# Turning k with 32x32 block transposes on VectorE and sixteen transfers, in place of two TensorE transposes

## The reference

```
q, k = rotary(x @ Wq), rotary(x @ Wk);  v = x @ Wv;  g = silu(x @ Wg)
per chunk of 64 tokens:  attn  = (q @ k.T) * decay          # k is contracted over its 64 columns
                         o     = attn @ v + (q * cross_q) @ S
                         S_new = gamma^64 * S + (k * cross_k).T @ v
x1  = layernorm(x + (rmsnorm(o) * gn_weight * g) @ Wo)
out = layernorm(x1 + (silu(x1 @ Wgate) * (x1 @ Wup)) @ Wdown)    # integer weights times 1/127, hidden width 768
```

## Time and profile before

| | value |
|---|---|
| median of three runs | 423.6 us |
| the profiled execution's own time | 423.2 us |
| its span (first to last instruction) | 421.5 us |
| PE busy | 412.1 us (98%), 4698 matmuls |
| DVE busy | 313.2 us (74%), 912 instructions |
| ACT busy | 268.2 us (64%) |
| POOL busy | 183.2 us (43%) |
| packets of the SP transfer queue q1 | 14144, 19.08 MB |

### The profile page before, as it was taken

The page is one execution under the profiler, slowest core; times in us unless marked ns, Lnnn a source line. Parts: engine busy times, 40 slices in busy tenths (PEclk is TensorE's granted clock), DMA queues, the critical chain, the costliest instruction groups (busy, mean ns, idle before and its releaser), DMA issues.

```text
span 421.5 us, 12747 instructions
## 1 busy us (share of the span) xinstructions
PE 412.1 (98%) x4698; PEld 394.4 (94%) x4698; DVE 313.2 (74%) x912; ACT 268.2 (64%) x812; POOL 183.2 (43%) x330
## 2 busy tenths in 40 slices
PE   8999999998999999999999999999999999999994
PEld 6899999998999999999999999999999999998994
DVE  4999776677777777867777867777777777784975
ACT  6678655577666766766766766666666666654551
POOL 2532344355344455334355344445443434442654
PEclk9999999999999999999999999999999999999999
DMA  8931010101020201102020110201110010100001
GB/s 284 360 131 52 0 51 2 53 14 39 12 68 2 76 2 40 39 2 77 2 55 25 40 40 2 76 2 40 39 26 29 2 51 2 40 14 15 15 25 55
DMA packets 14352, 19.99 MB, mean 47 GB/s; under 512 B 1488, under 2 KB 9808, under 8 KB 14288
## 3 DMA queue, kind: packets, MB, share of 16 engines
q1 hardware_dynamic: 14144, 19.08, 14.1%
q10 hardware_dynamic: 144, 0.07, 0.1%
HBM read 14.94 MB, written 4.19 MB: 45 GB/s over the span
## 4 chain that ended last, share of the span: by engine, by line
PE 94%; DVE 2%; DMA 1%; issue 1%; POOL 1%; ACT 0%; SPq 0%; POOLq 0%; DVEq 0%; ACTq 0%
PE b_rows L527 30%; PE b_rows L545 20%; PE b_ffn L527 20%; PE b_turn L763 3%; PE b_head L793 3%; PE b_head L801 3%; PE b_turn L558 2%; PE b_state L820 2%; PE b_ffn L711 2%; PE b_head L722 2%; PE b_head L814 1%; PE b_rows L541 1%; DMA wf_int<-in_w_proj 1%; PE b_head L689 1%; PE b_head L685 1%
## 5 line engine op out<-in xcount | busy, mean ns | idle before, releaser
L2032 POOL TENSOR_TENSOR h_lo<-wf_int,h_hi 128x256 fp32r<-128x256 f32 x96 | 70.0, 742 | 121.7 <-ACT h_hi L1210 121.7
L527 PE MATMUL b_ffn<-x1T_hi,wf_hi 128*128 128x256 f32 x384 | 92.0, 279 | 0.1
L527 PE MATMUL b_ffn<-x1T_lo,wf_hi 128*128 128x256 f32 x384 | 91.5, 278 | 0.0
L1199 ACT ACTIVATE wf_int<-b_ffn 128x256 f32<-128x256 f32 x96 | 36.9, 384 | 59.5 <-PE b_ffn L527 59.4
L527 PEld LDWEIGHTS b_ffn<-x1T_hi,wf_hi 128*128 128x128 f32 x384 | 72.2, 188 | 0.6 <-DVE x1T_lo L1668 0.2
L527 PEld LDWEIGHTS b_ffn<-x1T_lo,wf_hi 128*128 128x128 f32 x384 | 72.2, 188 | 0.0
L545 PE MATMUL b_rows<-wp_hi,xT_hi 128*128 128x256 f32 x230 | 66.4, 289 | 1.2 <-issue 1.2
L545 PE MATMUL b_rows<-wp_hi,xT_lo 128*128 128x256 f32 x244 | 66.5, 277 | 0.0
L545 PE MATMUL b_rows<-wp_lo,xT_hi 128*128 128x256 f32 x230 | 63.8, 277 | 0.0
L1608 DVE TENSOR_TENSOR wf_int<-b_ffn,wf_int 128x256 f32<-128x256 f32 x96 | 40.2, 419 | 26.3 <-ACT wf_int L1199 25.7
L1186 ACT ACTIVATE sq<-b_head 128x128 f32<-128x128 f32 x120 | 33.3, 278 | 28.7 <-PE b_head L801 19.6
(11 more groups left out here) (191 smaller groups left out, 1166.5 us busy)
## 6 DMA issues: line engine op xcount, KB each, us to landing
xT_raw<-in_xT SPq DMA_DIRECT2D x16, 256.0 KB, 2.8
x_sb<-in_x SPq DMA_DIRECT2D x16, 256.0 KB, 3.0
out<-wf_int SPq DMA_DIRECT2D x30, 128.0 KB, 1.8
wf_int<-in_w_ffn SPq DMA_DIRECT2D x6, 384.0 KB, 6.7
wf_int<-in_w_proj SPq DMA_DIRECT2D x6, 256.0 KB, 4.7
rope_sb<-in_rope SPq DMA_DIRECT2D x4, 256.0 KB, 5.7
rope_q<-in_rope_by_row SPq DMA_DIRECT2D x2, 512.0 KB, 9.5
wo_raw<-in_w_o SPq DMA_DIRECT2D x1, 512.0 KB, 6.4
```

The lines of the kernel that those rows point to most:

```text
L527: mm = pe.matmul(dst, a, b, start=(i == 0 and j == 0 and not begun), stop=(i == n - 1 and j == len(passes) - 1 and not more), skip_group_c ...
L1199: act.activation(act_g[:, u], b_ffn[u][:, 0:256], ACT.Silu, scale=SCALE).then_inc(silu_done[j], 1)
L2032: pool.tensor_tensor(h_lo[:, ring, hb], h_full[:, u], h_hi[:, ring, hb].bitcast(F32), ALU.subtract).then_inc(h_split[j], 1)
```

## The change

Tiles 9 to 30 (`moved`) no longer go through PE and ACT. Right behind `sum_k`, DVE transposes each 32x32 block of k in place in the grid of blocks, into a new buffer `k_blocks` (a part of a buffer that is free by then). SP then issues sixteen transfers inside SBUF for each tile, one for each pair of source quadrant i and destination quadrant j, that put the blocks where the turned k wants them. Each transfer reads 32 partitions and writes 32 partitions, with two runs of 32 elements (128 bytes) in each. `heads_ready` waits for all sixteen. `turn_qk` and `keep_qk` fall away for these tiles; `turn_y` loses its wait for the copy, except in two places; `sum_k` loses its wait for `qkT_done`; and the DVE transpose waits until the sixteen transfers of the tile before have landed.

```diff
+        k_blocks = wf_int[:, 5 * 512:5 * 512 + 256].bitcast(F32)
+        def moved(n):
+            return PACKED <= n < NT - 1
+        def moves(n):
+            return 16 * (P // BLOCK) ** 2 * (n - PACKED + 1)
+        def turned_before(n):
+            return min(n, PACKED)
...
+            def move_k(n):                                   # SP
+                blocks = k_blocks.rearrange("p (b j c) -> p b j c", b=2, c=BLOCK)
+                sp.wait_ge(k_blocked, n - PACKED + 1)
+                sp.wait_ge(scores_done, n)
+                for i in range(P // BLOCK):
+                    src = slice(i * BLOCK, (i + 1) * BLOCK)
+                    for j in range(P // BLOCK):
+                        sp.dma_start(qkT[j * BLOCK:(j + 1) * BLOCK, 2:4, src], blocks[src, :, j, :]).then_inc(k_moved, 16)
...
                 slot(s, s // TS, s % TS)                     # SP, s in range(NT)
+                if moved(s):
+                    move_k(s)
...
                     if n + 3 > PACKED:                       # turn_y
-                        pe.wait_ge(qkT_kept, min(n + 3, NT))
+                        if n + 3 == PACKED + 1 or n + 3 >= NT:
+                            pe.wait_ge(qkT_kept, turned_before(n + 3) + (1 if n + 3 >= NT else 0))
...
                 n, m = s - 1, s - 2                          # heads_ready
-                pe.wait_ge(qkT_kept, n + 1)
+                if moved(n):
+                    pe.wait_ge(k_moved, moves(n))
+                else:
+                    pe.wait_ge(qkT_kept, turned_before(n) + 1)
...
-                turn_qk(s, q, t)                             # PE, end of packed_slot
+                if not moved(s):
+                    turn_qk(s, q, t)
...
-                if exists(n):                                # ACT, keep_qk
-                    act.wait_ge(qkT_done, n + 1)
+                if exists(n) and not moved(n):
+                    act.wait_ge(qkT_done, turned_before(n) + 1)
...
-                    dve.wait_ge(qkT_done, s - 1)             # DVE, sum_k
+                    if not moved(s - 2):
+                        dve.wait_ge(qkT_done, s - 1)
...
+            def block_k(n):                                  # DVE
+                dve.wait_ge(rotated, n + 1)
+                if n > PACKED:
+                    dve.wait_ge(k_moved, moves(n - 1))
+                dve.transpose(k_blocks, qk[:, n % 2, 256:512]).then_inc(k_blocked, 1)
...
                 sum_k(s, q, t)                               # DVE, packed_slot
+                if moved(s):
+                    block_k(s)
                 add_q(s, q, t)
```

More of the change, by code:

```diff
@@ L57 @@
 CHUNKED = PACKED - 1
+BLOCK = 32
 def rope_tables():
@@ L229, in build_block @@
         qkT_done, qkT_kept = sem("qkT_done"), sem("qkT_kept")
+        k_blocked, k_moved = sem("k_blocked"), sem("k_moved")
         v_copied, g_gated = sem("v_copied"), sem("g_gated")
```

## The result

| | before | after |
|---|---|---|
| median, 4 runs each | 423.76 us (423.06 to 424.33) | 520.39 us (517.3 to 522.82) |
| span of the profiled execution | 421.5 us | 515.6 us |
| mean granted clock of TensorE | 1.00 in the packed stage | 0.91 in the packed stage, 0.931 over the span |

The ratio is 1.2277, with a 95% interval of 1.2193 to 1.2362: 96.6 us slower. The prediction was 435.0 us, at most 450. The sign and the way in which the time is lost were forecast; the size was not: 96.6 us against the 11.4 of the forecast, more than eight times as much.

The account below looks back on a forecast made before the run. PE was taken to bound the kernel, with k's longer way stalling it 0.68 us in most slots. 16.28 us of stalls added less 4.84 removed gave +11.4, so 435.0 us; range 418.5 to 450.

Parts of the forecast that it names:

- Sixteen issues: SP issuing a tile's transfers: 0.43 us for the first, then 14 x 0.48 = 6.72 us to the sixteenth's start.
- d: Distance between starts of successive transfer issues on SP: taken as 0.48 us, ends 0.39 and 0.54.
- landing: Last transfer of a tile, from the start of its issue until it lands: 1.5 us, ends 1.2 and 2.1.
- first issue: SP's opening transfer of each tile's burst: 0.39 + 0.04 = 0.43 us.
- L: Time along k's way from one gate (PE's wait before `attention_out`'s last matmul) to the next: 12.93 us against 12.25.
- block transpose: DVE's added transpose of k behind `sum_k`, 128x256 float32: 0.42 us.
- last semaphore: From the last transfer's semaphore to the weight load on PE at the gate: 0.1 us.
- The removed transposes: Two PE transposes of L558 per tile, 0.22 us a slot, 22 tiles: 4.84 us gained, all on the path.
- Gate to `sum_k`: From PE's weight load for `attention_out`'s last matmul to the end of `sum_k` on DVE: 3.69 us.
- B: Rival: each SP issue pays twice for its second loop, 0.535 us apart; +28.4, about 452 us; chance 0.20.
- C: Rival: SP issue cost goes with rows, some 0.40 us apart; burst hidden, kernel faster, about 419 us; chance 0.19.
- D: Rival: issues about 0.45 us apart, stall eats the gain, within 3 us of before; chance 0.11.

Follow-up runs that it names:

- sixteen stores: Changed kernel with its sixteen transfers per tile aimed at an HBM scratch buffer instead of `qkT`, turned k of tiles 9 to 30 left out: 452.59 us, ratio 1.0692.
- PE kept busy: Changed kernel with fourteen matmuls on a constant operand put on PE ahead of the wait for the moves: 507.68 us, ratio 1.198.
- the first two experiments: Changed kernel without the sixteen transfers and their waits (420.15 us), and with only the eight of source quadrants 0 and 1 (420.17 us).

## Why the prediction was right in sign and wrong in size

The step that failed is **"Sixteen issues"**: d was taken as 0.48 us with ends of 0.39 and 0.54, and it is 0.597 for the issue and 0.04 behind it, 0.638 from start to start. All rows that it was read from the earlier trace rows are transfers with one end in HBM. The arithmetic on them was sound (the sixteen stores measured 0.47), but the prediction argued about rows and loops, and neither matters; the end that did differ, SBUF on both sides, was noted for the landing ("No transfer inside SBUF is in this trace") and not for the issue. Its range of d was narrow because it varied the wrong property. The stated ends of 0.39 and 0.54 do not hold 0.638. This step alone, with the first issue 2.41 us a slot or 53 us, turns the forecast of 435 into 488; stretched issues, clock and landing make up the rest.

The mean slot, term by term:

| term | us |
|---|---|
| L as predicted | 12.93 |
| distance of issues, 14 x (0.638 - 0.48) | 2.21 |
| first issue, 0.59 + 0.04 for 0.43 | 0.20 |
| landing, 1.78 for 1.5 | 0.28 |
| stretched issues, 11.6 us / 22 | 0.53 |
| lower clock between gate and `sum_k` (4.20 - 3.67, the means without and with PE kept busy) | 0.53 |
| sum | 16.68 |
| measured | 16.74 |

Twenty-two times 16.74 - 12.93 is 84 us; with the +11.4 of the prediction that is about 95, and 96.6 were measured. The experiment with PE kept busy gives the term of the clock a second time: its slots last 16.22 us in the mean, 0.52 less. Two small terms nearly cancel: the block transpose, 0.445 for 0.42, and the last semaphore, 0.04 us for 0.1. No row of the trace before had shown the 0.1.

- **The removed transposes**, 4.84 us: 3.8 measured (2.7 to 4.8), by the kernel without transfers. Its slots last 12.26 us for 12.45. The two pieces are gone, but sixteen matmuls of `gate_up` take 1.89 us in place of 1.81 in nine of its packed slots, and did so in two before. Why was not tried.
- **L against PE's slot, and a stall in each slot if L is longer**: right, shown by eight transfers (420.17), twelve (451.99) and sixteen (520.4). The chain after has each step in the order given. The point from which it decides, 0.431 us for sixteen, was not met by a run; by number of transfers it lies between eight and twelve, and both sides were seen.
- **The block transpose at 0.42 us**: 0.445, and free of cost by the first two experiments, since both run at the 12.26 to 12.29 us of a PE that never waits. So were the later `add_q` and `mask`; the loads of `xT` and `x` were nobody's wait.
- **Gate to `sum_k`, 3.69 us**: right only at full clock (4.20 us in the mean of the changed kernel). "PE's stop would not shorten it" holds, but the stop lengthened it, because the clock fell in the gap and the first matmuls behind it ran up to twice as long. The prediction did not ask what an engine does after it has stood still.
- **The rivals.** B had the direction (dearer issues) with the wrong cause and too low a price, 0.535. C and D needed 0.45 or less, which not even a burst with one end in HBM has (0.47); the 0.427 us that the prediction gives beside C is met by issues with one end in HBM (0.427 to 0.432 without the gap) and by none inside SBUF. The dearest case that had a sum came to 452 us, since none had a price outside the rows; all of the bad ends together, over 470, were left out of the range, and even they come to an estimated 473 by its own terms.
- **Stretched issues** stand in no term of the sum, though the trace of before has one: the 1608 ns in the earlier trace rows, which the prediction did not weigh. While SP was idle most of the time they cost nothing; in a chain that runs through SP each counts in full.

## What to carry to other kernels

Where many small transfers come between a producer and its consumer, count issues first: the issuing time of the burst, and not its bytes, is the length of the path, and a burst is free only while this path is shorter than the work that covers it. A price read from transfers with an end in HBM does not hold for transfers inside SBUF; if a kind of operation is not in the trace, list what differs (place, rows, loops) and let each widen the range. And when a change can make TensorE stand still, price the work just behind the gap at the lower clock, and see whether a few larger transfers by way of HBM do the same with less.

## What the runs showed of the hardware

- An issue on SP takes 0.43 us back to back with one end in HBM and 0.59 to 0.62 us with both in SBUF, for 32 or 128 partitions and one or two runs; about 0.04 us lie between two. The Trainium skill (DMA: Bandwidth & Descriptors, Why small descriptors are slow (HBM only)) excepts transfers inside SBUF from its penalty on small descriptors. No run here measures that bandwidth; in the issue itself they are the dearer ones.
- SP and ACT issue at the same time without slowing each other noticeably: eight each in 5.07 and 5.41 us, with medians of 0.64 and 0.65 us from start to start, against 0.64 for SP alone.
- Now and then an issue is stretched. In the changed kernel 19 of 352 lasted 0.66 to 1.61 us in all, where 0.60 is usual. Of these, 18 overlapped an instruction-fetch packet of 8 KB or more, against 35 of the other 333; with sixteen stores it was 18 of 18 against 26 of 334, and the 1608 ns store of the kernel before overlapped one too. The queues in the 1.6 us before the long issue shown above; the packet of q8 starts at 276.9 us and lasts 1.4 us, and so runs into the issue that starts at 277.06:

```profile
q1 hardware_dynamic: 198, 0.02, 8.6%
q8 instruction: 1, 0.02, 5.6%
```

  This is a coincidence in time; no run removed the fetches, and so the cause stays open.
- Transposes of 32x64 float32 from one quadrant to another cost DVE 0.249 us apiece in a row, of which 0.236 is the instruction: sixteen of them cost nine times one of 128x256.
- The granted clock falls in some of the gaps of PE (the one shown is about 3.6 us) from 1.00 to 0.50, and the recall behind it takes 1.08 us for 0.61; with the gap filled by 14 matmuls it stays at full and the kernel is 12.7 us faster.
